# Cross-attention: GpSimd's elementwise work on VectorE, LayerNorm and router over more steps, eight score rows

## The reference

```
q = (x @ W_q); k = (context @ W_k); v = (context @ W_v)      # 8 heads of 64
sim = where(mask, einsum('bihd,bjhd->bhij', q, k) * 64**-0.5, -max)
out = einsum('bhij,bjhd->bihd', softmax(sim), v) @ W_o + b_o
x = x + out
# then: LayerNorm(x), router scores = softmax(xf @ w_router), top 2 of 8 experts
# slots by a running count per expert (capacity 896), experts, x + their sum + bias
```

## Time and profile before

| | |
|---|---|
| median of 3 runs | 3491.22 us |
| profiled execution, its own time | 3495.34 us |
| its span, from the first to the last instruction | 3493.6 us |
| mean granted TensorE clock | 0.943 |
| TensorE busy | 3107.0 us, 89% |
| VectorE busy | 1690.5 us, 48% |
| ScalarE busy | 1403.8 us, 40% |
| GpSimd busy | 726.0 us, 21% |

### The profile page before, as it was taken

The page is one execution under the profiler, slowest core; times in us unless marked ns, Lnnn a source line. Parts: engine busy times, 40 slices in busy tenths (PEclk is TensorE's granted clock), DMA queues, the critical chain, the costliest instruction groups (busy, mean ns, idle before and its releaser), DMA issues. The chain is left out here.

```text
span 3493.6 us, 52659 instructions
## 1 busy us (share of the span) xinstructions
PE 3107.0 (89%) x19340; PEld 2532.3 (72%) x19340; DVE 1690.5 (48%) x3672; ACT 1403.8 (40%) x2345; POOL 726.0 (21%) x564
## 2 busy tenths in 40 slices
PE   5888898958989988999999957999999999999997
PEld 4667777746777767777777735888788878888886
DVE  5888888843555555555555532333233322323232
ACT  5777777624555555555555521111111111111111
POOL 0000000001111121111111113242424242423343
PEclk9899999978999999999999977999999999999999
DMA  2111111122111111111111002131313131313132
GB/s 92 32 37 46 42 42 42 45 68 100 36 41 35 35 45 54 35 35 35 35 41 35 16 27 102 49 97 55 87 53 91 49 91 49 101 53 89 55 85 58
DMA packets 96194, 193.83 MB, mean 55 GB/s; under 512 B 18656, under 2 KB 28640, under 8 KB 94016
## 3 DMA queue, kind: packets, MB, share of 16 engines
q1 hardware_dynamic: 80912, 160.78, 14.9%
q0 software_dynamic: 15152, 31.26, 4.2%
HBM read 144.19 MB, written 47.82 MB: 55 GB/s over the span
## 5 line engine op out<-in xcount | busy, mean ns | idle before, releaser
L1612 DVE CAST f_hh<-f_hf 128x448 fp32r<-128x448 f32 x256 | 116.9, 457 | 891.7 <-ACT f_hf L1636 859.1
L1636 ACT ACTIVATE f_hf<-f_h 128x448 f32<-128x448 f32 x256 | 139.6, 545 | 1015.8 <-PE f_h L1672 987.6
L1688 PE MATMUL f_y<-f_w2h,f_hh 128*128 128x512 f32 x896 | 357.9, 399 | 0.0
L1559 POOL TENSOR_TENSOR f_w1l<-f_raw,f_w1h 128x512 fp32r<-128x512 f32 x130 | 183.4, 1411 | 828.5 <-DVE f_w1h L1594 828.3
L1688 PE MATMUL f_y<-f_w2h,f_hl 128*128 128x512 f32 x896 | 354.1, 395 | 0.0
L1688 PE MATMUL f_y<-f_w2l,f_hh 128*128 128x512 f32 x896 | 352.3, 393 | 0.0
L1247 ACT COPY c_pT<-c_psum 125x672 f32<-125x672 f32 x256 | 184.2, 719 | 311.7 <-PE c_psum L1353 309.9
L1255 ACT ACTIVATE c_s_sb<-c_s_sb,c_nmx 112x750 f32<-112x750 f32 x256 | 236.0, 922 | 161.9 <-DVE c_nmx L1091 159.0
L1672 PE MATMUL f_h<-f_xTh,f_w1h 128*128 128x448 f32 x1024 | 262.2, 378 | 32.5 <-ACT f_hf L1636 16.8
L1353 PEld LDWEIGHTS c_psum<-c_ident,c_s_sb 112*125 112x125 f32 x1536 | 204.1, 198 | 84.4 <-issue 78.1
L1672 PE MATMUL f_h<-f_xTl,f_w1h 128*128 128x448 f32 x1024 | 256.0, 372 | 0.0
(11 more groups left out here) (243 smaller groups left out, 5970.0 us busy)
## 6 DMA issues: line engine op xcount, KB each, us to landing
f_raw<-in_w SPq DMA_DIRECT2D x132, 512.0 KB
c_craw<-in_ctxT SPq DMA_DIRECT2D x16, 1125.0 KB, 5.5
a_x_in<-in_x SPq DMA_DIRECT2D x9, 896.0 KB, 5.6
a_xr<-in_x SPq DMA_DIRECT2D x8, 896.0 KB, 5.9
x_dram<-a_xr SPq DMA_DIRECT2D x8, 896.0 KB, 4.8
q_dram<-a_q SPq DMA_DIRECT2D x32, 224.0 KB, 5.3
c_q<-q_dram SPq DMA_DIRECT2D x16, 448.0 KB, 5.2
c_x<-x_dram SPq DMA_DIRECT2D x16, 448.0 KB, 5.6
```

The costliest lines, as they stand in the source:

```text
L1559: pool.tensor_tensor(w1s[1][:, n % NSLOT].rearrange("p k c -> p (k c)"), raw1[:, g % 2, n % 2, :], w1s[0][:, n % NSLOT].rearrange("p k c - ...
L1612: dve.tensor_copy(hs[0][:, l % 2, c * HC:c * HC + HC], hf[:, c, :]).then_inc(h_hi, 1)
L1636: act.activation(hf[:, c, :], H[:, 0:HC], ACT.Gelu_apprx_tanh).then_inc(free, 1)
L1688: mm = pe.matmul(Y[t][:], hs[a][:, l % 2, 128 * t:128 * t + 128], w2s[b][:, l % NSLOT, :], start=j == 0 and q == 0, stop=j == FB - 1 and q ...
```

## The change

GpSimd's three kinds of elementwise work go to VectorE: the low part of the context (one chunk in each of steps 5, 6 and 7), b_o (step 14) and the bias of the output (step 9). ScalarE casts one chunk of the context in each of steps 4, 5 and 6. PLAN is rearranged: OUT in steps 4 and 6, XT in 9 and 10, RT in 12, PRE in 15; K(0, 0) stays in step 7, now behind the transposes. VectorE's residual is in 5 and 7, LayerNorm in 8, routing in 13 and 15. `s_sb` has 8 rows, and the wait on the transposes is gone. In odd steps VectorE masks before it normalises. ScalarE's cast of PV(0) moves to step 6 and waits for OUT(1). A semaphore is renamed (q_madeaded to q_loaded).

```diff
-        s_sb = sb("s_sb", [R, 4, J])
+        NS = 8
+        s_sb = sb("s_sb", [R, NS, J])
...
-        PLAN = {0: ([], [K(3, 1)], []), 1: ([], [PV(3)], [V(1, 0)]), 2: ([], [V(1, 1)], []), 3: ([], [V(1, 2), OUT(0)], []),
-                4: ([], [OUT(1)], []), 5: ([], [PV(0)], []), 6: ([], [XT(0)], []), 7: ([K(0, 0)], [K(0, 1)], [XT(1)]),
-                8: ([], [K(1, 0)], []), 9: ([], [PV(1)], [RT]), 10: ([], [V(0, 0)], []), 11: ([K(1, 1)], [K(2, 0)], []),
-                12: ([], [V(0, 1)], []), 13: ([], [PV(2)], [PRE]), 14: ([], [V(0, 2)], []), 15: ([K(2, 1)], [K(3, 0)], [])}
+        PLAN = {0: ([], [K(3, 1)], []), 1: ([], [PV(3)], [V(1, 0)]), 2: ([], [V(1, 1)], []), 3: ([], [V(1, 2)], []),
+                4: ([], [OUT(0)], []), 5: ([], [PV(0)], []), 6: ([], [OUT(1)], []), 7: ([], [K(0, 0)], [K(0, 1)]),
+                8: ([], [K(1, 0)], []), 9: ([], [PV(1)], [XT(0)]), 10: ([], [XT(1)], [K(1, 1)]), 11: ([], [V(0, 0)], [K(2, 0)]),
+                12: ([], [RT], []), 13: ([], [PV(2)], [V(0, 1)]), 14: ([], [K(2, 1)], []), 15: ([], [PRE], [V(0, 2), K(3, 0)])}
...
# GpSimd: split_context, add_bias and the output's bias are taken out; left is
+            def send(i):
+
                 wait_apart(pool, slots_made, i)
                 for q in range(4):
                     pool.indirect_dma_start(out=table_dram, ...)
...
# VectorE
+            def lo_of_context(i, k):
+                dve.wait_ge(c_hi, i * CC + k + 1)
+                dve.tensor_tensor(cT[1][:, k, :], craw[:, k, :], cT[0][:, k, :].bitcast(F32), ALU.subtract).then_inc(c_lo, 1)
+
+            def add_bias(i):
+                dve.wait_ge(x_loaded, i * 16 + 16)
+                dve.tensor_tensor(x1[:], x1[:], bo[:, None, :].broadcast_to([R, 2, C]), ALU.add).then_inc(x1b_made, 1)
+
+            def with_bias(i):
+                dve.wait_ge(out_stored, i * 16 - 16)
+                dve.tensor_tensor(xo[:], x1[:], bi[:, None, :].broadcast_to([R, 2, C]), ALU.add).then_inc(xo_made, 1)
...
             def masked_ready(i, h):
 
-                dve.wait_ge(s_full, i * (NH // 2) + h // 2 + 1)
-                if h % 2 and not (isinstance(i, int) and i * NH + h - 3 <= 0):
-                    dve.wait_ge(pt_full, i * NH + h - 3)
+                if h % 2 == 0:
+                    dve.wait_ge(s_full, i * (NH // 2) + h // 2 + 1)
...
             def tail(i, kind, s):
-                if s in (3, 4):
-                    residual(i, kind, s - 3)
-                elif s == 5:
+                if s in (5, 7):
+                    residual(i, kind, s // 7)
+                elif s == 8:
                     layernorm(i)
-                elif s == 10:
+                elif s == 9:
+                    with_bias(i)
+                elif s == 13:
                     routing(i, kind, 0)
-                elif s == 14:
+                elif s == 14 and kind != "end":
+                    add_bias(i)
+                elif s == 15:
                     routing(i, kind, 1)
...
-                    if s in (6, 10, 14):
+                    if s in (7, 10, 14):
                         lo_of_outputs(i, kind, (s - 6) // 4)
                     elif s == 2 and kind != "first":
                         lo_of_outputs(i - 1, kind, NM - 1)
+                    if s % 2 and has_step(kind, s + 2):
+                        masked(*step(i, s + 2))
...
                     if has_step(kind, s + 1):
                         normalise(*step(i, s + 1))
-                    if has_step(kind, s + 2):
+                    if s % 2 == 0 and has_step(kind, s + 2):
                         masked(*step(i, s + 2))
+                    if s in (5, 6, 7) and kind != "last":
+                        lo_of_context(i + 1, s - 5)
...
# ScalarE
-                if s == 4:
+                if s == 7:
                     act.wait_ge(mv_made, i * 2)
...
-                elif s in (7, 8):
-                    unit = XT(s - 7)
+                elif s in (10, 11):
+                    unit = XT(s - 10)
...
-                elif s == 10:
+                elif s == 13:
                     act.wait_ge(gen_free[BANK[kind, RT]], uses_before(i, kind, RT) + 1)
...
-                    if s == 4 and kind != "last":
-
-                        act.wait_ge(gen_full, number(ORDER, i, kind, V(1, 2)) + 1)
-                        hi_of_context(i + 1)
-                    if s in (5, 9, 13):
+                    if s in (4, 5, 6) and kind != "last":
+                        if s == 4:
+                            act.wait_ge(gen_full, number(ORDER, i, kind, V(1, 2)) + 1)
+                        hi_of_context(i + 1, s - 4)
+                    if s in (6, 9, 13):
+                        if s == 6 and kind != "first":
+
+                            act.wait_ge(gen_full, number(ORDER, i, kind, OUT(1)) + 1)
                         hi_of_outputs(i, kind, (s - 5) // 4)
...
# TensorE: waits of the first scores of a turn
+                    if s == 15 and kind != "last":
+                        made(i, kind, K(2, 1))
                     for unit in units(kind, s, (2,)):
                         unit_of(i, kind, unit)
-                if kind != "last":
-                    made(i, kind, K(1, 1))
```

More of the change, by code:

```diff
@@ L944, in load_queries @@
             def load_queries(i):
-                sp.dma_start(q2[:], flat(one(q2_dram, i), "p k t")).then_inc(q_madeaded, 16)
+                sp.dma_start(q2[:], flat(one(q2_dram, i), "p k t")).then_inc(q_loaded, 16)
             load_context(0)
@@ L1040, in tail @@
                                             in_=pay[:, q, :], in_offset=None, bounds_check=E * CAP - 1, oob_is_err=False).then_inc(sent, 16)
-            split_context(0)
             pool.wait_ge(small_loaded, 48)
-            add_bias(0)
             pool.wait_ge(trash_stored, 16 * 15)
[L1047 to L1056, removed]
+            with pool.Fori(1, B + 1) as i:
+                send(i)
         @block.vector
@@ L1076, in normalise @@
                 dve.wait_ge(rec_made, i * NH + h + 1)
[L1077 removed]
+                dve.tensor_scalar(s_sb[:, h % NS, :], s_sb[:, h % NS, :], rec[:, h:h + 1], None, ALU.mult).then_inc(p_made, 1)
             def masked_ready(i, h):
[L1081 to L1083 removed]
+                if h % 2 == 0:
+                    dve.wait_ge(s_full, i * (NH // 2) + h // 2 + 1)
             def masked(i, h):
                 half = lambda t: t.rearrange("p (a j) -> p a j", a=2)
[L1087 removed]
+                nc.vector.tensor_tensor_reduce(out=half(s_sb[:, h % NS, :]), in0=score_view(h), in1=half(mb[:]),
                                                scale=1.0, scalar=-FLT_MAX, op0=ALU.add, op1=ALU.max,
@@ L1186, in tail @@
             def tail(i, kind, s):
-                if s in (3, 4):
-                    residual(i, kind, s - 3)
-                elif s == 5:
+                if s in (5, 7):
+                    residual(i, kind, s // 7)
+                elif s == 8:
                     layernorm(i)
-                elif s == 10:
+                elif s == 9:
+                    with_bias(i)
+                elif s == 13:
                     routing(i, kind, 0)
-                elif s == 14:
+                elif s == 14 and kind != "end":
+                    add_bias(i)
+                elif s == 15:
                     routing(i, kind, 1)
+            for k in range(CC):
+                lo_of_context(0, k)
+            add_bias(0)
             mask_of(0)
@@ L1229, in _, with hi_of_context @@
             act.wait_ge(const_set, 12)
-            def hi_of_context(i):
+            def hi_of_context(i, *ks):
                 act.wait_ge(c_loaded, i * 16 + 16)
-                for k in range(CC):
+                for k in ks:
                     act.copy(cT[0][:, k, :], craw[:, k, :]).then_inc(c_hi, 1)
             def copy_queries(i, g):
-                act.wait_ge(q_madeaded, i * 16 + 16)
+                act.wait_ge(q_loaded, i * 16 + 16)
                 act.copy(q[:, 2 * g:2 * g + 2], q2[:, 2 * g:2 * g + 2]).then_inc(q_made, 1)
@@ L1254, in exponential @@
                 act.wait_ge(nmx_made, i * NH + h + 1)
-                act.activation(s_sb[:, h % 4, :], s_sb[:, h % 4, :], ACT.Exp, bias=nmx[:, h:h + 1],
+                act.activation(s_sb[:, h % NS, :], s_sb[:, h % NS, :], ACT.Exp, bias=nmx[:, h:h + 1],
                                accum_out=den[:, h:h + 1]).then_inc(e_made, 1)
             def tail(i, kind, s):
-                if s == 4:
+                if s == 7:
                     act.wait_ge(mv_made, i * 2)
                     act.activation(rstd[:], mv[:, :, 1], ACT.Abs_reciprocal_sqrt, bias=eps[:]).then_inc(root_made, 1)
-                elif s in (7, 8):
-                    unit = XT(s - 7)
+                elif s in (10, 11):
+                    unit = XT(s - 10)
                     act.wait_ge(gen_full, number(ORDER, i, kind, unit) + 1)
-                    act.copy(xnT[:, s - 7, :], bank(kind, unit)[:, 0:KC * R]).then_inc(gen_free[BANK[kind, unit]], 1)
```

(8 more changed lines are left out.)

12 lines of the change are left out of this document (5 added, 7 removed).

## The result

The changed kernel takes **3515.55 us** (median of 12 runs, 3502.29 to 3528.48) against 3491.66 for the kernel before on the same chip (12 runs, 3487.88 to 3496.2). The ratio is 1.0066, with a 95% interval of 1.0049 to 1.0083: 0.66% slower. The forecast was 3495 with a range of 3455 to 3522; the time lies in the range, but outside the forecast case's own 3480 to 3510, beside rival D (3514). The profiled execution took 3516.84 (span 3515.1, 21.5 above the span before). Of the runs further on, one of e3's four (3556.29 us, at a granted clock of 0.824 where the other three had 0.958 to 0.961) was slow, and so was one of the kernel before, timed beside e1 to e4 (7861.44); without its slow run the median of e3 is 3346.78 and not 3348.76.

What follows compares the result with a forecast made beforehand. TensorE was taken to bound the kernel, through work, stalls and clock. 14 turns of +0.85 stalls and +0.35 clock gave +16.8, edges -13.1, together +3.7 on 3495.3; less 4.1 for the median: 3495 us, range 3455 to 3522.

Steps and rivals of the forecast that it cites:

- forecast case: Whole kernel: stalls move to K00, K11 and V00, with about two clock falls a turn; 3495 us, chance 0.47.
- rival D: Loop turns: each of the three long new stalls brings its clock fall at the full 1.7; 3514 us, chance 0.20.
- The stalls that go: TensorE's waits at step 2, step 6 (1.98), XT0 (2.27) and the 0.38 before a PV vanish; bias adds cost nothing.
- (1) K00: Step 7: K00 waits for VectorE's third split, ready 8.65 after step 6's scores start; stall 3.05 us a turn.
- (2) K11: Step 10: K11 waits for XT0's bank, which ScalarE copies after head 12's exponential; stall 2.45 us a turn.
- (3) V00: Step 11: V00 waits for XT1's copy, behind ScalarE's copy of probabilities and exponential; stall 2.4 us a turn.
- (4) V02: Step 15: K21 must be emptied before V02; stall 0.25 us a turn.
- Prices: GpSimd's work on VectorE: about 0.94 us a split and 1.23 a bias add, 5.3 us a turn.
- Rival E: VectorE: a long instruction keeps the engine longer than its row, the third split costing 1.80; 3507 us, chance 0.06.
- VectorE's load: Loop turns: VectorE some 5 us a turn busier, with 35 us a turn free.
- The edges: Outside the 14 turns: start -2.6, first batch +1, last batch -11, end -0.5; together -13.1 us.
- the clock: Loop turns: 2.2 falls of 1.7 us a turn instead of two, +0.35; bounds one fall (-1.7) and three (+1.7).

Runs made afterwards that it cites:

- e3: The changed kernel with ScalarE's copies to xnT first in steps 10 and 11 and the context split as early as before: 3348.76 us, 0.9587 of the kernel before.
- e1: The changed kernel with ScalarE's copies of XT0 and XT1 moved from the tail to the start of steps 10 and 11: 3399.0 us, 0.9729 of the kernel before.
- e4: The changed kernel with unused work in two stalls: 14 matmuls before K00's wait, XT1's transposes made six times over: 3449.9 us, 0.9881 of the kernel before.
- e10: The early-copies, early-split version of the changed kernel, with VectorE's two bias adds a turn cut to two columns: 3344.9 us, 0.9563 of the kernel before.
- e2: The changed kernel with the context split earlier, ScalarE's casts in steps 4 and 5, VectorE's thirds in 5 and 6: 3440.35 us, 0.985 of the kernel before.
- e11: The changed kernel with only K00's stall filled, by 14 matmuls whose result is not used: 3468.28 us, 0.9923 of the kernel before.
- e5: The changed kernel's order with GpSimd's splits (steps 4 to 6) and bias adds (9, 14) back on GpSimd: 3455.83 us, 0.9892 of the kernel before.
- e6: The kernel before with ScalarE's copies of XT0 and XT1 first in its steps 7 and 8: 3415.23 us, 0.9782 of the kernel before.
- e8: The changed kernel with only XT0's copy first in step 10, XT1's left where it was: 3432.77 us, 0.983 of the kernel before.

## Why the prediction was right, and where it was off

The range was right, and so was the walk through the orders; the likeliest case was not the one that came. Rival D came, by its mechanism in kind (every stall with its fall), and by its time (3514) partly by luck: D adds 0.85 of waiting and 1.7 of clock to a turn, and the runs show 0.15 and 2.4, two misses of 0.7 that cancel. In the forecast itself the same too large waiting (+0.7) covered a part of the too small clock (-2.0): a turn grew by 2.5 and not by 1.2.

- **The stalls that go**: all of them went, as predicted, and the bias adds cost TensorE nothing (e10). The reading behind one of them was off: the instruction of 2 columns that takes 2.27 us, which holds up xn, starts at 1306.13, beside GpSimd's x1 + bias (1306.04 to 1308.39) and not beside its splits. Both kinds of work left GpSimd, so the forecast doesn't change.
- **(1) K00**: 3.05 predicted, 2.90 measured; K00 starts 8.68 after the scores, 8.65 predicted. e2 shows the cause: one step earlier, and 0.37 is left. **(2) K11**: 2.45 predicted, 2.20 measured. **(3) V00**: 2.4 predicted, 2.14 measured. e1 shows the cause of both. **(4) V02**: 0.25 predicted, 0.41 measured. Their sum is 7.65 where 8.15 was predicted, and the stalls of before were 7.5 by the windows where 7.3 was taken: K01's 2.14 was read from one turn, and its mean is 2.5. So the waiting grew by 0.15 a turn and not by 0.85.
- **Prices**: a split 0.94 and a bias add 1.23 were estimated; the groups' means are 0.935 and 1.217. Rival E is excluded. The next instruction starts 0.86 after the split's start (1312.43 to 1313.29), before the split's row ends. The Trainium skill ("VectorE: DVE Perf Modes", The DRAIN you can't avoid) has a pause of about the duration less 266 ns, as an estimate 0.67 here, and adds that a next instruction that is not held starts earlier; the rows show no pause, and the prediction gave only the first half of what the section says.
- **VectorE's load**: 5 us a turn more was predicted, 0.7 came. The working had the 5.3 of added instructions and left out what it had itself read in the earlier trace rows, that VectorE's own instructions stretch beside GpSimd's: the normalise fell from 0.686 to 0.613 in the mean (16 a turn), and two instructions of 2 columns from 2.27 and 0.69 to 0.16 and 0.15, together 3.8 of the 4.6 that are missing. It made no difference to the time.
- **The edges**: -13.1 predicted, -13.5 measured (last batch -13.5 for -11, first batch +2.9 for +1, counted without the start's -2.5).
- **The step that failed is the clock**: +0.35 a turn was predicted, as 2.2 falls of 1.7 for two; 2.4 came (71.1 to 73.5 busy), 14 x 2.4 = 34 us, where 5 were allowed for. The bound I gave, three falls, +1.7, was itself too low. It took every fall at the same 1.7, read from one turn. The windows of three turns above and the table show that what a stall costs in clock does not follow from its length. e4 and e11 show that it is the idle time that brings the low clock, and no other property of the changed order: filled with useless work, the same turns run at 0.99 in e4, and 0.97 where only K00's stall is filled (e11), against 0.91. The same error stands behind the expectations for e2, e5 and e6, all of them too high by 18 to 39 us: each took the clock's price of before for a fixed one.
- The changed kernel's runs spread over 26 us where those of before spread over 8. The turns of one execution spread likewise (78.6 to 82.0 us), with the clock behind K00 at 1.00 or 0.72; that the runs differ for this reason is likely but was not shown.

**Open.** Which stall brings a low clock in which turn was not settled. It follows an order that no run here explains: in e8 three turns of 74.8 to 74.9 us are followed by one of 75.9 to 76.0, over and over, in e4 one or two of 75.8 by one of 77.3, and in e3, with nothing above 0.5 to wait for, every turn takes 69.4. And e6, with two stalls of 2 us within 5 us of each other, loses only 0.7, and e2, with two of 2.2 and 2.14 just as close, loses 2.7. The eight score rows were not tried by themselves; that they change nothing is only argued, from there being no wait for them in either kernel.

## What to carry to other kernels

Before work is moved to a faster engine, look at what stands ahead of it there: an engine that needs twice as long but has nothing else to do delivered the third split 1.6 us sooner. Copy a PSUM bank out at the start of a step, ahead of the exponential that waits for another engine: two moved lines gave 3.3% here, 2.2% in the old order. And price a stall of TensorE with the clock it loses, as a range: here from 0.2 us (V00's 2.14, e8 against e1) to 3.8 (K11's 2.2, after against e8). In this kernel the three stalls together cost 5.6 a turn in clock, where K00's alone cost 1.6 and the two others without it 2.7.

## What the runs showed of the hardware

- TensorE's granted clock went to its lower level behind stalls of only 2.1 to 2.9 us, in some turns and not in others with stalls equal to 0.01 us. A turn with 7.6 us idle lost 5.6 us of clock, one with 7.5 idle (before) lost 3.2, one with 5.4 idle 1.8, one with 1.2 idle 0.3.
- Products whose result nobody reads made the kernel faster: 14 of them a turn, 2.7 us, took 47 us off 3515.6.
- In the kernel before, a VectorE instruction of 2 columns ended with the GpSimd addition beside it, 2.27 us after its start; without GpSimd beside it, it takes 0.16. The two rows of before:
```profile
1306.13 2.27 DVE L1118 SCALAR_TENSOR_TENSOR c_nt<-c_mv,c_nt 112x2 f32<-112x2 f32 x1
1306.04 2.35 POOL L1032 TENSOR_TENSOR c_xo<-c_x,c_bi 112x1024 f32<-112x1024 f32 x1
```
